# A decoder layer on one core: the first feed-forward blocks are woven into the end of cross-attention

## The reference, cut to what matters

```
x = layernorm(x + self_attention(x))          # 16 heads of 128
x = layernorm(x + cross_attention(x, ctx))    # 16 heads of 128 and a rotary part of 64
y = quantise(x)                               # per token, to -128..127
h = quantise(silu(y @ Wg) * (y @ Wu))         # ternary weights, 1024 wide
out = layernorm(x + h @ Wd)
```

## Time and profile before

| | before |
|---|---|
| median of 3 runs | 1488.96 us (1488.28 to 1490.38) |
| profiled execution | 1488.86 us, its span 1486.8 us |
| granted TensorE clock, mean | 0.991 of full speed |
| PE / DVE / ACT / POOL busy | 93% / 80% / 84% / 85% of the span |
| self-attention, cross-attention, feed-forward | to about 973, to 1364, to the end |

### The profile page before, as it was taken

One profiled execution on the slowest core, in us unless ns is written; L12 is line 12 of the kernel. 1 busy time (PEld: TensorE's weight loads), 2 busy tenths in 40 slices (PEclk: granted clock), 3 DMA queues, 4 the chain that ended last, 5 costly groups with the idle time before them and its releaser, 6 DMA issues. The chain is left out here.

```text
span 1486.8 us, 54028 instructions
## 1 busy us (share of the span) xinstructions
PE 1375.3 (93%) x19830; PEld 1031.8 (69%) x20034; DVE 1196.8 (80%) x2796; ACT 1256.0 (84%) x4059; POOL 1269.5 (85%) x1307
## 2 busy tenths in 40 slices
PE   6999999999999999999999999868999999987897
PEld 3677777777777777777777777636777777765554
DVE  4887887887888878788787777878888888874997
ACT  6888888888888888888888888769999999996797
POOL 5889999999889899899898898658888899883887
PEclk9999999999999999999999999989999999999999
DMA  7700000000000000000000000023443433330012
GB/s 257 193 8 31 31 3 31 22 11 31 3 31 31 3 31 31 2 31 23 11 17 3 17 3 2 6 72 94 115 111 112 111 94 96 99 87 1 1 44 71
DMA packets 58132, 73.25 MB, mean 49 GB/s; under 512 B 14320, under 2 KB 41776, under 8 KB 57872
## 3 DMA queue, kind: packets, MB, share of 16 engines
q1 hardware_dynamic: 57872, 69.79, 15.7%
HBM read 32.54 MB, written 4.19 MB: 25 GB/s over the span
## 5 line engine op out<-in xcount | busy, mean ns | idle before, releaser
L663 DVE SCALAR_TENSOR_TENSOR X<-projP,r,X 128x256 f32<-128x256 f32 x512 | 211.2, 475 | 0.1
L305 PEld LDWEIGHTS svP<-W,xT 128*128 128x128 bf16 x3072 | 182.4, 98 | 31.9 <-DVE scores L650 2.5
L305 PE MATMUL svP<-W,xT 128*128 128x128 bf16 x3072 | 192.9, 219 | 0.4 <-DVE scores L650 0.4
L739 POOL TENSOR_TENSOR y_sql<-y_sq 128x512 bf16<-128x512 f32 x128 | 133.5, 1043 | 66.7 <-ACT y_sq L466 66.4
L256 PE MATMUL qkssP<-xT,W 128*128 128x512 bf16 x641 | 161.7, 383 | 29.5 <-issue 20.0
L256 PE MATMUL kP<-xT,W 128*128 128x512 bf16 x768 | 188.6, 382 | 0.2 <-DVE kl L696 0.2
L481 ACT ACTIVATE probs<-scores,ntop 128x64 f32<-128x64 f32 x512 | 170.5, 339 | 9.6 <-DVE ntop L653 9.6
L336 PE MATMUL projP<-W,y 128*128 128x256 bf16 x1024 | 175.9, 274 | 2.1 <-POOL yl L739 2.1
L1230 ACT ACTIVATE x_probs<-xsP,x_ntop 128x64 f32<-128x64 f32 x512 | 152.2, 325 | 19.3 <-DVE x_ntop L1307 18.5
L739 POOL TENSOR_TENSOR k_sql<-moved_k 128x512 bf16<-128x512 f32 x128 | 135.7, 1060 | 24.5 <-ACT moved_k L492 23.5
L938 POOL TENSOR_TENSOR qhl<-qh 128x1024 bf16<-128x1024 f32 x64 | 121.2, 1893 | 34.3 <-issue 23.3
(11 more groups left out here) (281 smaller groups left out, 4890.9 us busy)
## 6 DMA issues: line engine op xcount, KB each, us to landing
x_turned<-x_turn SPq DMA_DIRECT2D x128, 128.0 KB, 2.1
oB<-oA SPq DMA_DIRECT2D x232, 64.0 KB, 2.0
w_stage<-in_wqkvp SPq DMA_DIRECT2D x16, 512.0 KB, 3.6
x_stage<-in_xT SPq DMA_DIRECT2D x8, 512.0 KB, 4.1
X<-in_x SPq DMA_DIRECT2D x1, 4096.0 KB, 16.8
x_stage<-in_ctxT SPq DMA_DIRECT2D x8, 512.0 KB, 4.2
out<-X SPq DMA_DIRECT2D x7, 512.0 KB, 3.0
okv<-in_L_xattn_W_o SPq DMA_DIRECT2D x1, 2048.0 KB, 12.0
```

Of the source, the lines that this page charges most:

```text
L305: last = nc.tensor.matmul(svP[:, b * D:(b + 1) * D], xT[:, u, c, t * TILE + b * P:t * TILE + (b + 1) * P], weight(parity, z, 2, c), start= ...
L663: last = nc.vector.scalar_tensor_tensor(acc, projP[:, b * C:(b + 1) * C], r[:, PB + b:PB + b + 1], acc, ALU.mult, ALU.add)
L739: return nc.gpsimd.tensor_tensor(dst[:, :], src[:, :], high(src, slice(None), 0, TILE), ALU.subtract)
```

## The change

The two program parts become one. The first 67 slots of cross-attention (`CUT` = 67) run as before; then every engine walks one mixed list, in which "c" is a slot of cross-attention and "f" one of the feed-forward:

c67, f0, c68, c69, f1, c70, f2, c71, c72, f3, f4, ... f35

```diff
+    LAST, CUT = N + PROJ_AT, N + S_AT
+    order = [("c", CUT), ("f", 0), ("c", CUT + 1), ("c", CUT + 2), ("f", 1), ("c", CUT + 3), ("f", 2), ("c", CUT + 4), ("c", CUT + 5)]
...
+    def blocks(slot, lags, drain):
+        for kind, n in order + [("f", n) for n in range(1 + max(n for kind, n in order if kind == "f"), NB + lags)]:
+            if kind == "c":
+                drain(n)
+            else:
+                slot(n, lambda lag: 0 <= n - lag < NB)
```

`drain(n)` is cross-attention's own `slot(n)` of that engine. The inside of the slots of both kinds, and its order, stays, but for these moves:

```diff
# PSUM: gP, uP now lie over the four banks of latP, ropeP and sP, hmP over ptP and oP
+    gP, uP = front[:, 0:DFF], front[:, DFF:2 * DFF]
+    tP = [bank_[:, :].bitcast(F16) for bank_ in pair]
+    FREE = {s_g: ((used["s_lat"], pairs), (used["s_qh"], pairs - 1)), s_u: ((used["s_qh"], pairs), (used["s_exp"], pairs))}
# SBUF: sig, hs, hm, hqT lie in the dead weights, ds, xs and statistics in the dead mask
# ACT: the root of tile 6 (slot 68) goes
-                if g == 4 and 0 <= u < NT:
+                if g == 4 and 0 <= u < NT - 2:
# ACT: the sigmoid's table is loaded ahead of c67
# DVE: gsc, usc of blocks 0 to 23 ahead of c67; those of tile 6 join those of tile 7
+            own = slice(0, NB - 2 * PB)
# POOL: the root of tile 6, after the low half, in c68
+                if n == CUT + 1:
+                    own = slice((NT - 2) * PB, (NT - 1) * PB)
+                    wait(pool, s_mom, (NT - 1) * PB)
+                    nc.gpsimd.tensor_scalar(rstd2[:, own], moments[:, own, 1], EPS, None, ALU.add).then_inc(s_lastp, 1)
+                    nc.gpsimd.tensor_scalar(shift2[:, own], moments[:, own, 0], -1.0, None, ALU.mult).then_inc(s_lastp, 1)
+                    wait(pool, s_lastp, 3)
+                    nc.gpsimd.tensor_tensor(rstd2[:, own], rstd2[:, own], ffn["power"][:, :], ALU.pow).then_inc(s_lastp, 1)
+                    wait(pool, s_lastp, 4)
+                    nc.gpsimd.tensor_tensor(shift2[:, own], shift2[:, own], rstd2[:, own], ALU.mult).then_inc(s_shift2, 1)
# DVE: the sum of tile 7 stands behind c72 instead of ahead of f0
+            if n == order[-1][1]:
+                wait(dve, used["s_proj"], pairs)
+                nc.vector.tensor_tensor(acc, projP[:, :].rearrange("p (b c) -> p b c", b=PB), acc, ALU.add).then_inc(s_last, 1)
# tile 7 and the last quantisations come three slots later
-                if 1 <= n < 1 + PB:                    (DVE, statistics)
+            if 4 <= n < 4 + PB:
-                if n == 5:                             (POOL, root)
+            if n == 8:
-                if 6 <= n < 6 + PB:                    (ACT, layernorm)
+            if 9 <= n < 9 + PB:
-                if n == 11:                            (DVE, largest value; the scales 12 -> 15)
+            if n == 14:
-    XS_AT, XQ_AT = {6: (1, 2), 7: (12, 13)}, {6: 4, 7: 15}
+    XS_AT, XQ_AT = {6: (4, 5), 7: (15, 16)}, {6: 7, 7: 18}
```

More of the change, by code:

```diff
@@ L99, in build @@
         ffn = ffn_buffers(sb, ternary)
[L100 to L104, removed]
+        with ExitStack() as part:
+            cross_attention(nc, a, X, norm1, late, kept, ffn, out, sem, lambda n, s, d: sb(n, s, d, part), part)
 def self_attention(nc, a, X, norm, ident, eps_col, late, ternary, kept, sem, sb, part):
@@ L968, in qc_product, with cross_attention @@
     return last
-def cross_attention(nc, a, X, norm, late, kept, ffn, sem, sb, part, tail):
+def cross_attention(nc, a, X, norm, late, kept, ffn, out, sem, sb, part):
     kept = {**kept, "identb": sb("identb", [P, P], BF16)}
@@ L1003, in ps @@
         return part.enter_context(nc.psum_tensor(name, [P, n], F32))
[L1005 to L1007 removed]
+    projP, front = ps("xprojP", PB * C), ps("xfrontP", 4 * TILE)
+    latP, *ropeP, sP = (front[:, i * TILE:(i + 1) * TILE] for i in range(4))
+    ptP, oP = ps("xptP"), ps("xoP")
     s_latP, s_ropeP, s_s, s_pt, s_o, s_proj, s_step = (sem("c_" + n) for n in ("latP", "ropeP", "s", "pt", "o", "proj", "step"))
@@ L1053, in output @@
         return oB[:, m % 2, :]
+    s_last, s_lastp = sem("f_last"), sem("f_lastp")
+    used = {"s_lat": s_lat, "s_qh": s_qh, "s_exp": s_exp, "s_ptl": s_ptl, "s_oe": s_oe, "s_proj": s_proj, "s_xinv": s_xinv, "pairs": N}
+    order = [("c", CUT), ("f", 0), ("c", CUT + 1), ("c", CUT + 2), ("f", 1), ("c", CUT + 3), ("f", 2), ("c", CUT + 4), ("c", CUT + 5)]
+    programs = feed_forward(nc, X, ffn, late, projP, front, (ptP, oP), order, used, s_last, s_lastp, out, sem, sb)
     with nc.Block() as block:
@@ L1085, in _ @@
                     load_ctx(j + 3)
+            programs["sp"](sp)
         @block.tensor
@@ L1115, in other, with slot @@
                 last.then_inc(s_step, 1)
-            for n in range(LAST):
+            def slot(n):
                 if has(n, S_AT):
@@ L1188, in _ @@
                 other(n)
+            for n in range(CUT):
+                slot(n)
+            programs["pe"](pe, slot)
         @block.scalar
@@ L1283, in _ @@
                         last.then_inc(s_ln2, 1)
+            for n in range(CUT):
+                slot(n)
             nc.scalar.preload_act_table_set("sigmoid_and_others")
+            programs["act"](act, slot)
         @block.vector
@@ L1362, in _, with slot @@
                         nc.vector.reciprocal(xinv[:, own], xsc[:, own]).then_inc(s_xinv, 1)
-            done = slice(0, NB - PB)
-            nc.vector.tensor_scalar(ffn["gsc"][:, done], xsc[:, done], wsc[:, 0:1], None, ALU.mult)
-            nc.vector.tensor_scalar(ffn["usc"][:, done], xsc[:, done], wsc[:, 1:2], None, ALU.mult)
+            for n in range(CUT):
+                slot(n)
+            own = slice(0, NB - 2 * PB)
+            wait(dve, s_sc, NT - 2)
+            nc.vector.tensor_scalar(ffn["gsc"][:, own], xsc[:, own], wsc[:, 0:1], None, ALU.mult).then_inc(s_last, 1)
+            nc.vector.tensor_scalar(ffn["usc"][:, own], xsc[:, own], wsc[:, 1:2], None, ALU.mult).then_inc(s_last, 1)
+            programs["dve"](dve, slot)
         @block.gpsimd
         def _(pool):
-            for n in range(LAST):
+            nc.gpsimd.memset(ffn["power"][:, :], -0.5).then_inc(s_lastp, 1)
+            wait(pool, s_lastp, 1)
+            def slot(n):
                 j, g = divmod(n, HP)
@@ L1426, in _ @@
                     low_of(nc.gpsimd, qhl[:, m % 3, :], qh[:, m % 3].rearrange("p b i t -> p (b i t)")).then_inc(s_ql, 1)
-    return projP
+            for n in range(CUT):
+                slot(n)
+            programs["pool"](pool, slot)
 def ternary_buffers(sem, sb):
@@ L1482, in bank @@
         return tP[k % 2], sum(kind == "h" for kind, _ in front), sum(kind == "x" for kind, _ in front)
[L1484 to L1516, removed]
@@ L1533, in _ @@
[L1533 to L1558, removed]
-                                             ACT.Copy, bias=-MAGIC16).then_inc(s_xqT, 1)
-                if 6 <= n < 6 + PB:
-                    i = NB - PB + n - 6
-                    x = X[:, i, :]
-                    wait(act, s_lastp, SHIFT)
-                    nc.scalar.activation(x, x, ACT.Identity, bias=shift[:, i:i + 1], scale=rstd[:, i:i + 1]).then_inc(s_xqT, 1)
-                for e in NORMED[n]:
-                    x = X[:, e, :]
-                    wait(act, s_shift, e // GROUP + 1)
-                    nc.scalar.activation(x, x, ACT.Identity, bias=shift[:, e:e + 1], scale=rstd[:, e:e + 1]).then_inc(s_by_act, 1)
-            NORMED = [[e for e in range(MAIN) if min(e + 10, NB + 3) == n] for n in range(NB + 4)]
-            blocks(slot, 4)
```

354 lines of the change are left out of this document (208 added, 146 removed).

## The result

The change made the kernel slower: 1505.22 us median (1504.0 to 1506.4, 4 runs) against 1488.83 us (1488.28 to 1490.38, 4 runs), a ratio of 1.0117 with a 95% interval of 1.0103 to 1.0131. The profiled execution took 1506.4 us with a span of 1504.6 us and a mean granted clock of 0.985 (before 0.991). PE, DVE and POOL are busy 94%, 80% and 85% of the span, nearly the shares of before: the page hardly shows that 16 us were lost.

A forecast was written before the change was run, and what follows sets the result against it. The prediction saw idle engines in the drain, a chain of copy, POOL's low half and projection, and DVE pacing the feed-forward behind it. 9.4 + 3.0 + 3.7 = 16.1 us on 1488.96 gave 1505, range 1502.5 to 1508.

The forecast's parts named there:

- The yardstick and the chain: From slot 67's last projection matmul to block 3's `hs`: round trips in sequence, 35.5 us against 26.1, so 9.4 later.
- The clock: PE's idle gaps in the mixed slots: the clock falls to 0.50 behind them, costing 3.7 us more.
- the two places named: PE's waits for POOL's low half in c70 and c71, over 5 us each, with a clock of 0.50 behind.
- the long place: Profile at 975 to 980 us, clock 0.50 after 5.37 us of idleness; by it the two gaps cost 4.8 us.
- between the two places: Two earlier profile readings of the slow clock after idleness, pricing the two gaps at 2.6 or 4.8 us.
- The middle: Price taken for the slow clock behind PE's two gaps: 3.7 us, between 2.6 and 4.8.
- The rival that it is hidden: In PE's gaps the clock holds or its price hides beside another engine's wait: 12.4 us more, 1501.4; chance 0.25.
- Behind block 3: From block 3's `hs` to the end: tile 7's later work, refill and layernorms add about 3.0 us (1.1, 1.3, 0.4, 0.3).
- The sum: Whole kernel: 9.4 + 3.0 + 3.7 = 16.1 us more, added to the median 1488.96 for 1505.
- What was costed at nothing: In and around the drain: delayed `x_ptl` of c68, added waits, new SBUF and PSUM places, one `memset`: no visible cost.
- Slower still, over 1510: Near f8 and the refill: POOL may not catch up and the clock may fall again; over 1510 us, chance 0.06.
- The one for a faster kernel, 1482.3: The drain absorbs blocks 0 to 2, block 3's `hs` near 1366: 6.7 us faster, 1482.3; chance 0.10.

The follow-up runs named there:

- the kernel with a busy PE: The changed kernel plus 22 unread 512-column matmuls in each of PE's two long waits, in c70 and c71: 1501.55 us, ratio 1.0090 to the kernel before.
- the dose (none to three blocks): The changed kernel with no, one, two or three feed-forward blocks mixed among the drain slots: 1488.35, 1492.11, 1499.40, 1505.22 us.
- the reordered lists: The changed kernel with low halves ahead of block work on POOL's list: 1491.58 us; with DVE's `x_ptl` of c68 also ahead of block 0: 1484.93 us.
- the attempt to remove one: The changed kernel with tile 7's scaling on POOL one slot later and its transposition two: 1507.32 us, ratio 1.0127 to the kernel before.
- tile 7 late: The kernel before with tile 7's work and tile 6's scaling three slots later: 1493.00 us, ratio 1.0034 to the kernel before.

## Why the prediction was right, by its steps

**The yardstick and the chain** (9.4 us, and the clock within it): block 3's `hs` came 13.0 us later; 9.4 + 3.7 = 13.1 had been forecast. Link by link, from product to product: 12.7 forecast and 12.5 measured; 9.6 and 10.9 without the clock, and the kernel with a busy PE has 9.6 and 10.7; 2.3 to the `hs` and 2.27. The mechanism is shown by the dose (none to three blocks) and by the reordered lists, not only read from the trace. The forecast starts for `hs`, 1352.0, 1364.7, 1374.3 to 1375.5 and 1385 to 1389, were met but for block 2, at 1376.04, since its own product ran at the low clock.

**The clock** (3.7, between 2.6 and 4.8): 4.1 by the links, 4.4 at block 3, 3.7 by the medians. It fell at the two places named, to 0.50. How it is shared between the gaps comes out by comparing the change with the kernel with a busy PE. Behind the first gap, c70's projection took 1.1 us more and block 2 took 1.2 more from its product to its `hs` (3.39 for 2.21), together 2.2, as by the long place. Behind the second, c71's and c72's projections took 1.8 more: the clock came back during the second of them, so this gap lies between the two places. The middle was a choice and not a reading, and that it came so near owes something to luck. The rival that it is hidden (1501.4) is the kernel with the busy PE: 1501.55. By the rule of the Trainium skill that the prediction weighed ("TensorE: Matmul & The Clock Gate", section "What's actually happening"), the penalty is under 1% of a span; 4 us of 1505 agree. But they are a quarter of what this change did, so for a change the rows had to decide, as they did.

**Behind block 3** (3.0): the term that was mis-sized. It measured 4.85 in the trace, 4.1 when undone and 5.0 when made alone in the kernel before (3.8 by that kernel's trace). The parts that were foreseen came: block 3 to block 10 took 27.46 us against the 27.7 worked out, with a wait of 3.02 for a forecast 3.3. What failed is the sentence "from there both kernels walk the same slots, and the tail is the same". Ahead of block 10 PE stood still for 2.6 us, and the clock is at 0.83 from 1410 to 1420 (0.61 and 0.54 in the two stretches of 2 us from 1416 on), where it was 1.00 in the 5 us ahead of them and throughout the same stretch of the kernel before:

```profile
1405.00:1410.00 5.00, 4.49 (x39) 3.00 (x38) 4.79 (x12) 3.40 (x5) 4.14 (x10) 1.00 0.00 0
1410.00:1420.00 10.00, 7.38 (x42) 3.71 (x40) 6.58 (x11) 6.25 (x9) 7.97 (x17) 0.83 0.00 1
```

Block 12 waits 1.26 us behind it. And tile 7's scaling, also three slots later, loads POOL near the roots of f15 (0.55 and 1.59 us at blocks 18 and 19, where the kernel before waits 0.71 at block 16). From block 10 to 31 the kernel after takes 73.8 us for 71.4, so 2.4 us where 0.3 had been forecast. How that is shared among these waits stays open, since the attempt to remove one moved it.

**The sum**: 16.1 forecast; the medians differ by 16.4, the profiled spans by 17.8 (13.0 + 4.85). The profiled execution of the kernel after was the slowest of its four runs; that the median came out so near the forecast owes something to chance: by the traces the sum is 1.7 us short, nearly all of it behind block 3.

**What was costed at nothing** held as far as it can be told: `x_ptl` of c68 ran at 1354.42, as forecast (1354.7), with PE's transposition behind it, and POOL's chain hid it. But it is hidden only by that chain: with POOL's list mended and DVE's not, block 1 stayed at 1362.46, and moving `x_ptl` as well brought it to 1357.20 (POOL's list is the same up to block 0 in both).

**The rivals.** Slower still, over 1510, did not come. The one for a faster kernel, 1482.3, was wrong for this order of the lists and right about the room. (Its own sum, 1352 and 12.2, gives 1364.2 for block 3 and not 1366; the prediction doesn't say where the other 1.8 us come from.) It said that a link would have to cost under 6.9 us and that its place is POOL's low half. With the lists reordered the links between `hs` are 7.1, 3.7 and 5.8, 5.5 on average, and block 3 stands at 1366.7, near the 1366 of that rival.

## What to carry to other kernels

Where two pipelines are merged into one list, what counts on each engine is not how much idle time there is but what stands ahead of an instruction: one wait for the new work's round trip placed ahead of the old work's short step turns both into a chain. The engines need not walk the same order: putting each engine's short, already fed steps ahead of its wait for the round trip was worth 20 us here, with no instruction changed: it turned a loss of 16 us into a gain of 3. Also, what is moved by whole slots must be laid beside the periodic work of its new slots, here a group's roots every four blocks.

## What the runs showed of the hardware

- Idle time of PE has a second price. Two waits of 5.6 us each were followed by projections and products at a granted clock of 0.50, 4.1 us in all; 22 matmuls of 512 columns (4.91 us) in each wait, whose results nobody reads, kept it at 1.00, and the median was 3.7 us lower.
- Even a shorter wait of PE in mid-pipeline can bring this: behind 2.6 us of idleness ahead of block 10 the clock was 0.61 and 0.54 in the next two stretches of 2 us. It need not: behind the 2.7 us between the two parts the kernel before kept 1.00, and in the profile of the same kernel with tile 7 late it fell to 0.50 behind 2.5 us at the same place. So the clock behind a wait of this length is not a property of the kernel alone, and one profile doesn't settle it.
- The power on POOL costs 1.05 us for 128 x 4 numbers, as much as the low half of 128 x 512 (1.04).
